# Input-projection weights loaded once for two batches, and batch 1's x products placed ahead of the first scan, in a Mamba, cross-attention and feed-forward decoder layer

## What is computed

```
hidden = rmsnorm(residual) * norm_w
x, z   = split(hidden @ W_in)          # W_in: 512 x 2048, x and z: 1024 channels each
x      = silu(conv4(x) + conv_b)       # 4 taps along the 224 rows, per channel
dt_raw, B, C = split(x @ W_x)          # 64, 16, 16
dt     = softplus(dt_raw @ W_dt + b_dt)
h      = exp(dt*A) * h + (dt*x)*B      # a scan over the rows, 16 states per channel
y      = sum(h*C) + x*D
out    = residual + (y * silu(z)) @ W_out
```

## Time and profile before

| | |
|---|---|
| median of three runs | 3401.52 us (3398.46 to 3403.88) |
| profiled execution, its own time | 3404.25 us |
| span of that execution in the trace | 3402.7 us |
| mean granted TensorE clock | 0.969 of full speed |
| first scan starts | 61.94 us |
| batch 0's 32 slots end, batch 1's begin | 200.02 us |

### The profile page before, as it was taken

How to read it: one execution, slowest core, us unless ns; L and a number is a source line. 1 busy time by engine, 2 the same in 40 slices (tenths; PEclk the granted TensorE clock), 3 DMA queues, 4 the chain that set the end, 5 groups by cost and what they waited for, 6 DMA issues and landing times. The chain is left out here.

```text
span 3402.7 us, 59176 instructions
## 1 busy us (share of the span) xinstructions
PE 3155.0 (93%) x20736; PEld 2196.4 (65%) x20736; DVE 2577.2 (76%) x4546; ACT 2261.3 (66%) x5049; POOL 1737.7 (51%) x1194
## 2 busy tenths in 40 slices
PE   6699989998999999999998899999999999899999
PEld 5566656665567566666665566666666666578887
DVE  4799999999999999999986577777777777523232
ACT  4678777777777777777764577777777777622222
POOL 2678788788887888778875000100000000055554
PEclk8799999999999999999999899999999999999999
DMA  6677677676767767677665121211211221210100
GB/s 176 178 191 190 180 184 176 174 197 176 185 177 188 187 167 186 184 186 186 171 173 166 54 73 55 89 49 48 85 59 48 73 71 61 63 61 25 48 27 25
DMA packets 286725, 424.98 MB, mean 125 GB/s; under 512 B 28801, under 2 KB 226177, under 8 KB 281954
## 3 DMA queue, kind: packets, MB, share of 16 engines
q1 hardware_dynamic: 278957, 412.62, 44.3%
q10 hardware_dynamic: 7477, 8.59, 0.9%
HBM read 320.12 MB, written 101.02 MB: 124 GB/s over the span
## 5 line engine op out<-in xcount | busy, mean ns | idle before, releaser
L808 POOL TENSOR_TENSOR a_hs<-a_rep,a_bmat 128x896 f32<-128x896 f32 x512 | 1061.1, 2095 | 336.4 <-PE a_yps L319 323.6
L442 ACT ACTIVATE a_states<-a_rep,a_a_neg 128x224 f32<-128x224 f32 x2048 | 795.6, 439 | 194.8 <-DVE a_hs L708 181.9
L701 DVE TENSOR_TENSOR_SCAN a_states<-a_states,a_hs 128x900 f32<-128x900 f32 x384 | 779.0, 2029 | 100.1 <-ACT a_states L442 99.5
L1433 DVE CUSTOM_DVE_ANT_0 b_sc<-sps,early_mask 112x375 f32<-112x375 f32 x1024 | 499.6, 544 | 135.4 <-PE sps L1179 129.5
L1320 ACT ACTIVATE b_sc<-b_sc,b_nmax 112x750 f32<-112x750 f32 x512 | 467.3, 913 | 0.7 <-DVE b_nmax L1439 0.7
L1193 PEld LDWEIGHTS b_tps<-ident,b_sc 112*125 112x125 f32 x3072 | 357.3, 189 | 169.8 <-issue 118.7
L341 PE MATMUL a_work<-early_scan_hT,w_in 128*128 128x224 f32 x2048 | 432.1, 370 | 16.7 <-issue 13.2
L341 PEld LDWEIGHTS a_work<-early_scan_hT,w_in 128*128 128x128 f32 x2048 | 411.7, 202 | 42.0 <-issue 30.2
L1193 PE MATMUL b_tps<-ident,b_sc 112*125 112x112 f32 x3072 | 404.8, 281 | 26.8 <-DVE b_pT L1447 18.2
L708 DVE TENSOR_TENSOR a_hs<-a_states,a_cmat 128x896 f32<-128x896 f32 x384 | 419.0, 1091 | 13.2
L1573 POOL TENSOR_SCALAR b_x_var<-mv 112x2 f32<-112x2 f32 x16 | 3.4, 214 | 814.2 <-DVE mv L1484 814.2
(11 more groups left out here) (193 smaller groups left out, 4735.3 us busy)
## 6 DMA issues: line engine op xcount, KB each, us to landing
a_rep<-du_scratch SPq DMA_DIRECT2D x512, 224.0 KB, 5.5
w_in<-W_in_dram SPq DMA_DIRECT2D x128, 512.0 KB, 4.5
du_scratch<-early_du SPq DMA_DIRECT2D x15, 1792.0 KB, 6.5
ctx<-ctxT_dram SPq DMA_DIRECT2D x48, 500.0 KB, 5.8
v_scratch<-kv_out SPq DMA_DIRECT2D x96, 250.0 KB
k_scratch<-kv_out SPq DMA_DIRECT2D x96, 250.0 KB, 4.3
b_keys<-k_scratch SPq DMA_DIRECT2D x8, 1500.0 KB, 9.2
b_v<-v_scratch SPq DMA_DIRECT2D x8, 1500.0 KB
```

Of the source, the lines that this page charges most:

```text
L442: e = act.activation(rows(states[:, g % DA, :])[:, q, 1:ROW], rep[tile % REPS][:, j, 0, :], ACT.Exp, scale=a_neg[:, g % SLOTS, q:q + 1])
L701: dve.tensor_tensor_scan(state if g % G4 else whole, state, whole, 0.0, ALU.mult, ALU.add).then_inc(S["scan"], 1)
L808: pool.tensor_tensor(hs[g % RING][:, :, 1:ROW], rep[tile % REPS][:, j, 1, :].unsqueeze(1).broadcast_to([P, Q, L]), bmat[b % 2][:], ALU.mul ...
L1433: dve.tensor_tensor_reduce(out=sc[buffer_of(block)][:, j, cols], in0=sps[0:TT, j, 0:HALF], in1=mask[:, block % 2, cols], scale=-1.0, scala ...
```

## The change

- **Loads.** Eight blocks of W_in (x pairs 0 to 3, z pairs 0 to 3; "units" 0 to 7) are loaded once and serve batches 0 and 1. They lie in seven buffers: the two of `w_in`, four places that `wv`, `ctx` and `kv_out` use later, and `zs2`. Unit 7 takes buffer 0 again after batch 1's first x product. Units 0 and 1 are issued at once, 2 to 6 at slot -64, 7 at slot -34. From batch 2 on `load_w_in` goes on as before. Since the buffers are shared, the loads of `wk`/`wv` and of `ctx` at slot 6 gain a wait for an x or a z product, `keep_kv(0)` and `skip(1)` a wait for z products.
- **Batch 1.** Its normalised rows are transposed at slot -45 and copied at -43 (ahead of `keep_xd` of batch 0, into `yT[1]`), its x products stand at -38 to -35. The taps of pairs 0 and 1 stand ahead of the first scan, those of pairs 2 and 3 at slots -1 to 1. Its silu, `x_dbl`, `keep_xd` move from slots 11 to 13 to 5 to 7, its z products to 5, 6, 9, 10.
- **Batch 0.** All four z products come after those x products (-34 to -31), and their copies on ACT at slots 0 to 3.
- **Waits.** PE starts after four small transfers instead of eleven; the other seven have a semaphore of their own (`more_weights`). C has its own semaphore (`cc`), so slot 0 needs B alone. For batch 0, B is still issued by ACT, C by SP.
- **Order.** `softplus` of all four pairs stands together; `skip` of batch 0's second half goes to DVE; `store_du_first` of pair 0 and 1 is followed by `load_rep` of tile 0, then pair 2 and 3, C, `load_rep` of tiles 1 and 2, and unit 7.

```diff
+        self.w_first = [*self.w_in, *(mem.inside(f"w_first{i}", [P, D // P, 2 * P], start + at * row // 2)
+                                      for i, at in enumerate((4, 5, 6, 2)))]
...
+        hT_first = yT[1][:, 0:KD, :]
+        w_first = [*(tile[:] for tile in shared.w_first),
+                   zs[2][:].rearrange("p m l -> p (m l)")[:, 0:2 * P * KD].rearrange("p (k c) -> p k c", k=KD)]
...
-        n_weights = 11
+        n_weights = 4
+        n_more_weights = 7
...
         FIRST = {
...
-            "load_x": [-67, -66, -48, -47], "load_z": [-46, -45, -43, -7], "x": spaced(-49, 1), "tap": spaced(-48, 1),
-            "older_taps": spaced(-47, 1), "z": [-45, -38, -36, -2], "keep_z": [-39, -37, -35, 0], "residual": [-37],
+            "x": spaced(-49, 1), "tap": spaced(-48, 1),
+            "older_taps": spaced(-47, 1), "z": spaced(-34, 1), "keep_z": spaced(0, 1), "residual": [-49],
...
-            "softplus": [-40, -40, -38, -38], "skip": [-45, -39], "spread": [-38], "silu_z": [13],
-            "u": [-39, -39, -37, -37], "store_du": [-37]}
+            "softplus": [-40, -40, -40, -40], "skip": [-45, -42], "spread": [-37], "silu_z": [13],
+            "u": [-39, -39, -38, -38], "store_du": [-40, -40, -38, -38], "rep": [-39, -36, -35]}
         SECOND = {
-            "load": [-65], "row_stats": [-62], "squares": [-36], "guess": [-36], "gains": [-35], "h": [-34], "hT": [-1],
-            "keep_hT": [1], "load_x": [-6, 3, 5, 7], "load_z": [-5, 4, 6, 8], "x": spaced(2, 2), "tap": spaced(3, 2),
-            "older_taps": spaced(4, 2), "z": spaced(3, 2), "keep_z": spaced(4, 2), "residual": [9], "silu_x": [11],
-            "x_dbl": [12], "xd": [13], "store_bc": [13], "dt": [18, 18, 21, 21],
+            "load": [-65], "row_stats": [-62], "squares": [-52], "guess": [-48], "gains": [-48], "h": [-47], "hT": [-45],
+            "keep_hT": [-43], "x": spaced(-38, 1), "tap": [-34, -33, -1, 0],
+            "older_taps": [-33, -32, 0, 1], "z": [5, 6, 9, 10], "keep_z": [6, 7, 10, 11], "residual": [9], "silu_x": [5],
+            "x_dbl": [6], "xd": [7], "store_bc": [7], "dt": [18, 18, 21, 21],
...
             def project(b, name, pair):
                 pe.wait_ge(S["hT"], 2 * (b + 1))
...
+                if b < 2:
+                    unit = first_unit(name, pair)
+                    pe.wait_ge(S[f"w_first{unit}"], 16)
+                    weights, rows_T = w_first[unit % len(w_first)], hT_first if b else hT
...
             pe.wait_ge(S["weights"], 16 * n_weights)
-            pe.wait_ge(S["const"], n_const - 1)
...
+            def skip_first():
+                dve.wait_ge(S["xs"], 2)
+                dve.wait_ge(S["more_weights"], 16 * n_more_weights)
+                for m in range(M // 2, M):
+                    e = dve.tensor_scalar(yT[0][:, m, :], xs[:, m, :], d_skip[:, m:m + 1], None, ALU.mult)
+                e.then_inc(S["skip"], 1)
...
+            def load_w_first(name, pair):
+                unit = first_unit(name, pair)
+                if unit >= len(w_first):
+                    sp.wait_ge(S["x_ps"], PAIRS + 1)
...
             load_x(0)
+            load_w_first("x", 0)
+            load_w_first("x", 1)
...
+                if slot == -64:
+                    for name, pair in (("x", 2), ("x", 3), ("z", 0), ("z", 1), ("z", 2)):
+                        load_w_first(name, pair)
+                if slot == -34:
+                    load_w_first("z", 3)
...
                 if slot == 6:
+                    sp.wait_ge(S["x_ps"], 2 * PAIRS)
                     for dst, src in ((wk, t["Wk"]), (wv, t["Wv"])):
                         sp.dma_start(dst[:], src.rearrange("(k p) d -> p k d", p=P)).then_inc(S["w_kv_in"], 16)
+                    sp.wait_ge(S["z_ps"], PAIRS + 1)
                     load_ctx(0)
                     load_ctx(1)
```

More of the change, by code:

```diff
@@ L282, in products, with first_unit @@
             return (G4 - 1) * (g // G4) + g % G4
+        def first_unit(name, pair):
+            return pair + (PAIRS if name == "z" else 0)
         def in_unit(b, name, pair):
-            if b == 0:
-                return pair + (PAIRS if name == "z" else 0)
-            return 2 * (PAIRS * b + pair) + (name == "z")
+            return 2 * (PAIRS * (b - 2) + pair) + (name == "z")
         of_unit = {in_unit(b, name, pair): (name, PAIRS * b + pair)
-                   for b in range(B) for name in ("x", "z") for pair in range(PAIRS)}
+                   for b in range(2, B) for name in ("x", "z") for pair in range(PAIRS)}
+        of_unit[-2], of_unit[-1] = ("z", 2 * PAIRS - 1), ("x", PAIRS + 1)
         def rows(buffer):
@@ L348, in x_dbl @@
                     take_bank(("xd", b, 0), "bc", b + 1)
+                if b == 0 and part == 0:
+                    pe.wait_ge(S["more_weights"], 16 * n_more_weights)
+                    pe.wait_ge(S["const"], n_const - 1)
                 bank, last = bank_of["xd", b, 0], part == len(when[b]["x_dbl"]) - 1
@@ L473, in keep_hT @@
                         k = 2 * half + j
-                        e = act.activation(hT[:, k, :], work[:, bank_of["hT", b, half], j * L:(j + 1) * L],
+                        e = act.activation(dst[:, k, :], work[:, bank_of["hT", b, half], j * L:(j + 1) * L],
                                            ACT.Copy, scale=norm_w[:, k:k + 1])
@@ L561, in spread_first @@
                 act.wait_ge(S["bc_stored"], 16)
-                for first, tiles in ((0, bmat), (N, cmat)):
-                    for n in range(G4):
-                        act.dma_start(tiles[0][n * DG:(n + 1) * DG],
-                                      bc_dram[0, first:first + N, :].rearrange("(q n) l -> n q l", n=G4)[n]
-                                      .partition_broadcast(DG)).then_inc(S["bc0"], 16)
+                for n in range(G4):
+                    act.dma_start(bmat[0][n * DG:(n + 1) * DG],
+                                  bc_dram[0, 0:N, :].rearrange("(q n) l -> n q l", n=G4)[n]
+                                  .partition_broadcast(DG)).then_inc(S["bc0"], 16)
             def sum_piece(n):
@@ L646, in scalar_program @@
                 for b, half in due(slot, "skip"):
-                    skip(b, half)
-                if slot == FIRST["spread"][0]:
+                    if (b, half) != (0, 1):
+                        skip(b, half)
+                if slot == -38:
                     spread_first()
@@ L758, in vector_program @@
                 if slot == -57:
+                    dve.wait_ge(S["weights"], 16 * n_weights)
+                if slot == -43:
                     dve.wait_ge(S["a_exp"], 1)
-                    dve.wait_ge(S["weights"], 16 * n_weights)
+                    dve.wait_ge(S["more_weights"], 16 * n_more_weights)
                     dve.tensor_scalar(a_neg[:], a_neg[:], -1.0, None, ALU.mult).then_inc(S["const"], 1)
@@ L763, in vector_program @@
                     older_taps(b, pair)
+                if slot == FIRST["skip"][1]:
+                    skip_first()
                 for b, pair in due(slot, "u"):
@@ L804, in inputs @@
                 if g % SLOTS == 0:
[L805 removed]
+                    pool.wait_ge(S[f"bc{b % 2}"], 16 * G4 * (b // 2 + 1))
                 if g >= RING:
@@ L958, in sync_program @@
                 for b, _ in due(slot, "spread"):
-                    if b:
-                        spread_bc(b)
-                for b, _ in due(slot, "store_du"):
+                    spread_bc(b)
+                for b, pair in due(slot, "store_du"):
                     if b:
@@ L964, in sync_program @@
                     else:
-                        for pair in range(PAIRS):
-                            store_du_first(pair)
+                        store_du_first(pair)
+                for _, tile in due(slot, "rep"):
+                    load_rep(tile)
                 for b in range(B):
@@ L984, in sync_program @@
                     sp.dma_start(w_out[:], t["W_out"].rearrange("(m p) d -> p m d", p=P)).then_inc(S["w_out_in"], 16)
-                if 0 <= slot + 2 * G4 < ALL and slot % G4 == 0:
+                if G4 <= slot < ALL - 2 * G4 and slot % G4 == 0:
                     load_rep(slot // G4 + 2)
```

59 lines of the change are left out of this document (37 added, 22 removed).

## The result

The changed kernel took **3377.99 us** (median of four runs, 3376.67 to 3378.34) against 3402.49 for the kernel before beside it (3398.46 to 3403.88): a ratio of 0.9931 with a 95% interval of 0.9915 to 0.9947, 24.5 us less. The forecast was 3380.5 in a range of 3369 to 3391. The profiled execution took 3378.27 us with a span of 3376.6, so between the two profiled executions there are 26.0 us. The forecast gain was 21 us, so the change brought about a fifth more than that.

What follows compares the result with a forecast made beforehand. Steady batches run near the limit of DVE and PE, batch 0 does not. Gains of 8.2 us to slot 0, 12 and 0.5 in batch 0's halves, say 21, off 3404.25 give 3383.3; median 3380.5, range 3369 to 3391.

Steps and rivals of the forecast that it cites:

- PE's start: Ahead of the first scan: transposes, released by w_x at 14.66, wait for four small transfers instead; gain 2.65 us.
- signs that the sum is wrong: `keep_z` waiting in slots 0 to 3, pair 1's taps releasing scan one, batch 1 growing; idle over 1 us before slot 4.
- Main case: Whole kernel: 20.7, say 21 us gained, median 3380.5 us; alone 3374 to 3387; chance 0.62.
- rival B: Slots 16 to 32 also lose some 9 of 11.5 us excess; 30 us gained, 3371 us; chance 0.14.
- x pairs 2 and 3: Ahead of the first scan: their wait of 0.63 us for a buffer goes; gain 0.6 us.
- keep_hT ahead of keep_xd: Prologue, ACT: batch 1's four copies take 1.47 us, 0.8 within a wait, 0.7 paid; `keep_xd` near 37.1.
- From dt to rep: Prologue: store of pair 0 at 40.3, first rep issued at 43.4 instead of 48.07, 4.7 us earlier.
- rep and B to slot 0: Prologue: B and rep ahead of C and the last two stores, landing near 51.5; first scan 53.7, 8.2 us earlier.
- Slots 0 to 16: First half of batch 0: 13.0 us of stalls and taps go, ACT's two stalls of 6.3 us stay; net gain 12.
- Slots 16 to 32: Second half of batch 0: gain of 0.5 us taken, between nothing and 11.5.
- Rival A: First scan 3 us late with PE at 1.2 GHz, ACT's z copies cost 5.2 more; 12.8 us gained, 3389; chance 0.16.
- Rival C: Slots 0 to 16: slow z products make ACT's copies hold decays; 8 us behind at slot 32, 3409 us; chance 0.04.

Runs made afterwards that it cites:

- e1: Changed kernel with PE waiting at its start for all eleven small transfers again; 3383.6 us, one run.
- e9: Changed kernel with PE waiting for all eleven small transfers and weight blocks 2 to 6 issued only after those landed; 3378.0 us, one run.
- e5: Changed kernel with four blocks of W_in (2 MB) loaded once more at slots 1, 3, 5 and 7, without the old waits; 3379.0 us, one run.
- e6: Changed kernel with only batch 1's silu, x_dbl, keep_xd and store of B and C back at slots 11 to 13; 3381.9 us, one run.
- e12: The changed kernel itself, unaltered, run again beside the run with B on SP; 3379.32 us (3376.07 to 3386.03).
- e2: Changed kernel with all four stores of dt and dt*x on SP ahead of the first rep; 3378.4 us, one run.
- e3: Changed kernel with POOL's first input waiting for C as well as B; 3381.8 us, one run.
- e7: Kernel before the change with the loads of wk, wv and ctx (3 MB) at slot 10 instead of 6; 3399.05 us against 3402.26.
- e4: Changed kernel, weights still early, with batch 1's x products back at slots 2 to 8, z products at 3 to 9, silu to keep_xd at 11 to 13; 3385.8 us.

## Why the prediction was right

The account is the table at the top, step by step. The path that was forecast is the path that moved: PE's start, `keep_xd`, the stores, rep, POOL's first input and slot 0 each came within 0.8 us of the time given, the gain came in the prologue and the first half batch, and it went through to the end. Two of the prediction's own signs that the sum is wrong did appear: `keep_z` waited for PE in slots 1 to 3 (3.20, 5.16 and 1.03 us), and slot 4 had 1.02 us of idle time where no more than 1 was to be. Slot 16 came at 108.6 and slot 32 at 171.75, 4 and 7 us ahead of the times given. Main case and range hold the result; the measured 24.5 (26.0 in the profiles) lies about midway between the main case's 21 and rival B's 30.

*PE's start* (2.65 us forecast): 14.66 to 11.98, 2.7. What the prediction passed over is that the step is worth more within the change than against the kernel before. It said the blocks share the engines with w_x "which is not needed until `x_dbl`". That is so only because PE no longer waits for w_x. With the wait and the blocks queued ahead (e1), slot 0 comes 6.7 us later. With the wait alone (e9) it comes 1.75 us later than in the changed kernel's profile, 1.2 to 2.3 later than in the four, and nothing of it is left at slot 8. So the 2.65 us were gained at slot 0 and are worth nothing later on, as long as the blocks do not hold w_x up.

*x pairs 2 and 3, keep_hT ahead of keep_xd*: 37.03 against 37.1, so both terms, and the 0.7 us for the copy, were right in sum. (In e5, e6 and e12 it ran at 35.83, 37.23 and 36.68.) The four `skip` operations on DVE took 1.07 us, inside the bounds of 0 and 1.6, and DVE waited for softplus after them.

*From dt to rep, and rep and B to slot 0*: right in sum (8.3 against 8.2), by terms that were not, and the agreement to 0.1 us is luck. The sum was read off one profile of the old kernel, whose slot 0 at 61.94 is the latest of three; the four profiles of the changed prologue and the three of the old lie 5.5 to 8.9 us apart, 7.2 between the means. Rep's issue came 0.7 us earlier than forecast, and its landing 8.8 us after issue instead of 8.1. The bytes ahead of rep were priced alike at 215 to 224 GB/s; the stores cost 1.65 us for 0.9 MB (e2), while waiting for C cost 4.7 us (e3). The store order, to which the prediction gave a paragraph, is worth nothing at the end; the wait for C is worth about 4 (slot 32 in e3).

*Slots 0 to 16* (12 forecast, 16.4 measured) is the step that was mis-sized. The 13.0 us of removed stalls and taps were there: 2.31, 5.79 and 4.9. The term "I keep their two stalls, 6.3 us" is what failed: they came to 0.88 and 1.48 us, 3.9 less. I had kept them because the two pieces of ACT stay as long as they were. Their cost to DVE hangs on where they stand, and e6 shows it by putting the one back. The z copies were priced at 0.4 us ahead of slot 4, 1 us at most elsewhere; ahead of slot 4 they cost 1.02.

*Slots 16 to 32* (0.5 forecast, 3.6 measured): between the ends given, and what goes with it is the clock at slot 22, which the prediction had only as its rival B's "slow products". That it is the cause is argued from the match over 14 profiles. Rival B asked for 9 us here and did not happen.

Rival A did not happen in the profile above, where the clock was 1.00 from 41 to 53 us. But its premise, PE at its lower level after the pause, is a matter of the single execution, in both kernels. Pairs 2 and 3 of batch 0's `dt_raw` in the kernel before, and in e7, which runs the same code up to there (PE's timeline of each):

```profile
43.09 3.35 PE L362 MATMUL a_work<-a_xd,early_w_dt 65*128 65x224 f32 x8 [1.07 <-ACT a_zs L508]
```
```profile
42.66 1.78 PE L362 MATMUL a_work<-a_xd,early_w_dt 65*128 65x224 f32 x8 [1.07 <-ACT a_zs L508]
```

And the changed prologue's first two x products of batch 1 took 6.22 us in the changed kernel's profile and in e6, 7.48 in e12, and in e5:

```profile
41.22 8.10 PE L356 MATMUL a_work<-a_yT,w_in 128*128 128x224 f32 x32
```

Even in e5 slot 0 came at 54.13, released by POOL 1.29 us after the last taps, and not at 56.5. What A had wrong is how long the lower level lasts: it took both of these products at that level throughout, 11.4 us, and in no profile did they take over 8.5. Rival C's chain existed but held only one product at the lower clock. What slots 32 to 64 lost, 1.1 us, sits at slot 57, where the changed kernel waited 1.7 us and the one before did not.

Not shown by any run: whether loading once is needed at all. e5 puts back half the bytes, e4 all of the placement; a kernel that loads each block twice and still has the x products early was not tried.

## What to carry to other kernels

A piece of work moved ahead in a hand-ordered stream brings other pieces with it, and these can be a good part of the gain: here the long pieces on ACT cost DVE 5.4 us with the first at slot 11 and 2.4 us with it at slot 5. Before restructuring loads, look at what stands in front of the late one in its queue: one line, moving 3 MB of loads four slots later, removed the largest single stall within the old kernel's slots 0 to 32. And when transfers are queued early, check who still waits for a transfer that they will hold up.

## What the runs showed of the hardware that was not expected

- The same matmuls after the same pause run at either level of the clock: `dt_raw` after 2.7 us of idle took 1.78 us in one kernel and 3.35 in another, and one z product after 2.20 us took 4.95 or 3.27. In slots 16 to 32 the two groups of kernels lie about 2 us apart (63.2 to 64.1 against 65.1 to 66.7). The code alone does not fix the level: the same stream up to slot 0 gave 3.35 or 1.78 us for `dt_raw` (before, e7) and 6.22, 7.48 or 8.10 for two x products (after, e12, e5), and slot 0 differed by 1 to 2 us between such profiles.
- Ten matmuls of filling raised the clock from 0.74 and 0.50 to 1.00 in the windows where they stood and just after, and did nothing 25 us later.
- 0.9 MB of stores with 3.6 KB rows ahead of rep cost 1.65 us; 2.5 MB of weight blocks queued in SP's queue delayed a transfer in ACT's queue by 5.1 us (w_x at 19.34 against 14.25).
